# Second attention of a gated cross-attention stack: values and softmax sums in one product, normalised per query

## The chip, the cores and the metric

The kernel runs on one core of one Trainium2 chip. The metric is the device time of one execution in microseconds; lower is better. The engines are TensorE (PE in the profile; PEld is its weight load), VectorE (DVE), ScalarE (ACT), GpSimd (POOL) and SyncE (SP, which here only issues DMAs).

## The reference

Eight stages follow each other on x, of 16 items with 128 rows and 256 columns. Stages 0, 2, 4 and 6 are attentions over a context, stages 1, 3, 5 and 7 are feed-forward blocks; each adds its gated result to x. The change is in stage 2, the second attention:

```python
# q = layernorm(x), k = v = ctx_2048; per item B, rows D=128, columns L=256
qh = q.reshape(B, 8, 16, L)          # heads are groups of 16 ROWS
kh = k.reshape(B, 8, 16, L)
vh = v.reshape(B, 8, 16, L)
qk = jnp.einsum('bhdq,bhdl->bhql', qh, kh) / sqrt(16)
sm = jax.nn.softmax(qk, axis=-1)
ret = jnp.einsum('bhql,bhdl->bhdq', sm, vh).reshape(B, 128, L)
x = x + jnp.tanh(g_xattn[1]) * gamma * ret
```

So attention here runs between the 256 columns, and a head is 16 of the 128 rows. An item has 8 heads of 256 queries and 256 keys.

## The kernel before

The four compute engines and SyncE each run their own program, written out by hand, and wait on semaphores (`wait(name, item, k)` waits for the k-th signal of an item under that name). In stage 2 every engine walks the same loop, `s2_turns` (L2331): turns i = -3 to 17, and in one turn an engine handles several items at different steps. In names: b = i, p = i - 1, pp = i - 2, n = i + 3 on VectorE, GpSimd and SyncE, and n = i + 1 on TensorE.

An item goes through these steps:

- Preparation, for item n: VectorE combines the gathered rows of the stage before into x (L734) and takes the statistics (L772, L775). GpSimd makes the reciprocal deviation (L788, L790), normalises (L2385) and splits the result into three bf16 parts (`operands`, L804 to L812). SyncE stores the parts to `qscr` and loads them back as the operand `qop`, each of six combinations once (L2373), and the keys as `kop` (L2347). The keys of item n are loaded only after the key scores of item n - 3 are done. ScalarE scales gathered rows for a later item (`weigh`, L741), and GpSimd adds and gathers them (L748, L766).
- Maxima, for item b: TensorE makes scores by query in four steps (`scores`, L2540: 4 products each, two steps for each tile of 128 queries). VectorE takes each step's maxima per query and head (L2463), and splits the 16 maxima of a row into three bf16 parts (L804 to L812). TensorE transposes them into 24 rows of PSUM (L2600), and ScalarE copies these rows twice, for the even and the odd heads, into rows 96 to 119 of `qop` (L2516).
- Key scores, for item p: TensorE makes the scores again, keys on the partitions and with the maxima already subtracted, in four steps of 4 heads and 128 keys (`key_scores`, L2551). ScalarE takes the exponential of each step in two halves (L2504) into `PT`.
- Values, for item p: four steps (`values`, L2567). A step has 8 fp32 products of 128x32 by 128x256. Four of them multiply the exponentials with the values, laid out in `v2` as 32 columns of which 16 are those of a head and 16 are zero. The other four multiply them with `ones2`, 16 columns of ones, so that the sums stand in each of the 16 rows of a head. One product has two records in the trace. The even and the odd heads are added into one bank of PSUM: values in columns 0 to 255, sums in 256 to 511.
- End, for item pp: VectorE takes the reciprocal of the 128x256 sums (L2453) and multiplies the values with it and with the gate (L2459) into `q_tmp`. GpSimd adds `q_tmp` to x (L2406). x_done counts the items.

The order on each engine is fixed by the body of its loop. On TensorE one turn is: key scores 0 of p, scores 2 of b, key scores 1, values 0, scores 3, key scores 2, values 1, key scores 3, values 2, scores 0 of the next item, the transposes of the maxima of b (after a wait for them), values 3, scores 1 of the next item. On VectorE: maxima 0 and 1, preparation of n, the reciprocal of pp, maxima 2, the scaling of pp, maxima 3, the split of the maxima. On ScalarE: eight exponentials of p with the scaling of gathered rows behind the fourth, then both copies of the maxima of b. On GpSimd: the layout of the values of b (L2413, L2414, which waits for the values of b - 2), adding and gathering rows, deviation and normalisation of n, the addition for pp, the split of n. Behind the loop TensorE makes the context products of three items for stage 4 (L1295, L1298), which ScalarE copies (L1308, L1309). ScalarE then casts the weights w3h of stage 3 (L2176).

Two other places do what the change adds. In stage 0 ScalarE copies 128x512 of values and sums to `bc_sb` (L1023). In stage 4 TensorE transposes such a copy (L2962), and VectorE takes the reciprocal of 16 sums per row (L2776) and multiplies with it (L2778).

## Time and profile before

| | us |
|---|---|
| three runs | 1204.98, 1209.03, 1212.16 |
| median | 1209.03 |
| profiled execution | 1208.87 |
| its span, first to last instruction | 1207.1 |

| engine | busy, share of the span |
|---|---|
| TensorE, products | 86% |
| TensorE, weight loads | 67% |
| VectorE | 67% |
| GpSimd | 50% |
| ScalarE | 49% |

Busy shares are over all eight stages. The records of TensorE's products overlap, since one starts while the one before still runs out; its order and the distances of the starts say more than its busy time. Times in the rows are microseconds from the start of the span, where nothing else is said.

### The profile page before, as it was taken

To read this page: it belongs to the slowest core of one execution; us is meant where nothing else is said; L and a number is where in the kernel's file an instruction comes from. 1 tells how busy PE (TensorE), PEld (TensorE's weight loads), DVE (VectorE), ACT (ScalarE), POOL (GpSimd) and SP (SyncE) were. 2 spreads that over 40 slices of the span, in tenths; PEclk is the share of its full clock that TensorE was granted. 3 is DMA by queue.
4 is the path that set the end of the run, shared out by engine and by line. 5 is a ranking of instruction groups with operands and counts; after the bars stand their busy time and mean duration, and the time that the engine had idled before them with its cause. 6 is when DMAs were issued, how large, how long until landed. Compare 5 with 4: busy or idle time off the path is not lost.

```text
span 1207.1 us, 30765 instructions
## 1 busy us (share of the span) xinstructions
PE 1040.5 (86%) x11053; PEld 811.5 (67%) x11053; DVE 809.0 (67%) x2187; ACT 596.0 (49%) x1354; POOL 599.9 (50%) x1158
## 2 busy tenths in 40 slices
PE   4898899998687848888899979999978789879898
PEld 2576676766677724444577756777756589878898
DVE  2567666765555558888688875888765756745575
ACT  2455555655555347776621105777733544356432
POOL 2454656564688478874221114777643616600361
PEclk8899999999999969999999997999979989989999
DMA  5333333333566765544110011111021601244331
GB/s 181 98 99 103 102 99 100 121 125 126 182 210 204 177 166 143 145 135 115 41 70 0 1 42 31 35 36 35 4 87 51 212 2 62 80 124 154 105 113 60
DMA packets 110191, 119.85 MB, mean 99 GB/s; under 512 B 13373, under 2 KB 94485, under 8 KB 109789
## 3 DMA queue, kind: packets, MB, share of 16 engines
q1 hardware_dynamic: 96892, 89.65, 24.4%
q0 software_dynamic: 8256, 22.08, 6.2%
q10 hardware_dynamic: 4896, 6.20, 1.6%
q8 instruction: 89, 1.46, 0.5%
q14 instruction: 58, 0.47, 0.1%
HBM read 68.85 MB, written 49.03 MB: 98 GB/s over the span
## 4 chain that ended last, share of the span: by engine, by line
PE 50%; DVE 23%; issue 9%; DMA 7%; POOL 5%; ACT 4%; SPq 1%; ACTq 0%; POOLq 0%; DVEq 0%
PE psum L1125 4%; DMA PT<-xs 3%; DVE mx L2463 2%; DVE mx L888 2%; DVE x L2257 2%; PE psum L2567 2%; DVE mx L2764 2%; PE psum L1057 2%; PE psum L1758 2%; PE psum L1108 2%; PE psum L1760 2%; PE psum L1759 2%; PE psum L1059 2%; PE psum L1088 2%; PE psum L1969 2%
## 5 line engine op out<-in xcount | busy, mean ns | idle before, releaser
L888 DVE TENSOR_REDUCE mx<-psum 128x6 f32<-128x960 f32 (+3 forms) x80 | 80.7, 1008 | 65.4 <-PE psum L1093 64.3
L788 POOL TENSOR_SCALAR veps<-mv 128x1 f32<-128x1 f32 x112 | 28.8, 257 | 189.6 <-DVE mv L775 138.9
L766 POOL DMA_INDIRECT got<-ys,rows_y x64 | 63.9, 998 | 110.6 <-DMA ys<-yt 88.1
L975 ACT ACTIVATE PT<-psum 128x1024 f32<-128x1024 f32 x64 | 65.5, 1023 | 64.9 <-PE psum L1113 64.9
L2463 DVE TENSOR_REDUCE mx<-psum 128x4 f32<-128x1024 f32 x64 | 76.9, 1205 | 22.4 <-PE psum L2540 22.4
L2504 ACT ACTIVATE PT<-psum 128x512 f32<-128x512 f32 x128 | 69.5, 595 | 19.2 <-PE psum L2551 17.8
L1758 PE MATMUL psum<-xnTh,w7h 128*128 128x256 f32 x256 | 75.1, 293 | 1.3 <-issue 0.7
L1760 PE MATMUL psum<-xnTh,w7l 128*128 128x256 f32 x256 | 73.1, 286 | 0.0
L1759 PE MATMUL psum<-xnTl,w7h 128*128 128x256 f32 x256 | 73.0, 285 | 0.0
L2861 ACT ACTIVATE PT<-psum,mx 128x128 f32<-128x128 f32 x256 | 69.8, 396 | 5.1 <-DVE mx L2764 5.1
L790 POOL TENSOR_TENSOR rstd<-veps,minus_half 128x1 f32<-128x1 f32 x112 | 67.6, 604 | 9.3
L2567 PE MATMUL psum<-PT,arena 128*32 128x256 f32 x1024 | 70.0, 388 | 0.0
L1832 ACT ACTIVATE sil<-psum 128x256 f32<-128x256 f32 x64 | 24.5, 385 | 83.4 <-PE psum L1760 83.4
L2257 DVE SCALAR_TENSOR_TENSOR x<-psum,cw,x 128x256 f32<-128x256 f32 x128 | 52.4, 476 | 12.5 <-PE psum L2134 12.3
L1850 DVE TENSOR_TENSOR hTf<-sil,psum 128x256 f32<-128x256 f32 x64 | 26.7, 418 | 48.3 <-ACT sil L1832 48.0
L2132 PE MATMUL psum<-w3h,xnTh 128*128 128x512 f32 x128 | 53.1, 415 | 4.7 <-DVE x L2257 4.4
L2072 DVE TENSOR_TENSOR xTl<-psum,xTh 128x256 fp32r<-128x256 f32 x78 | 33.0, 424 | 31.8 <-ACT xTh L2043 31.1
L2868 ACT COPY arena<-psum 128x1024 f32<-128x1024 f32 x32 | 32.4, 1012 | 41.5 <-PE psum L2940 41.5
L1250 POOL COPY arena<-kv_f 32x64 f32<-32x64 f32 x160 | 38.7, 242 | 27.4 <-POOL arena L1250 22.1
L1969 PE MATMUL psum<-ident,PT 128*128 128x128 f32 x156 | 33.4, 297 | 21.6 <-DMA PT<-xs 20.2
L2085 DVE TENSOR_TENSOR ht<-silt,psum 128x128 f32<-128x128 f32 x78 | 22.4, 287 | 44.2 <-ACT silt L2055 43.9
L2134 PE MATMUL psum<-w3h,xnTl 128*128 128x512 f32 x128 | 50.9, 398 | 0.0
(445 smaller groups left out, 3473.7 us busy)
## 6 DMA issues: line engine op xcount, KB each, us to landing
xs<-qpad SPq DMA_DIRECT2D x34, 512.0 KB, 3.3
PT<-xs SPq DMA_DIRECT2D x78, 128.0 KB, 2.3
ys<-yt SPq DMA_DIRECT2D x78, 128.0 KB, 2.1
ext<-qscr SPq DMA_DIRECT2D x96, 64.0 KB
arena<-in_w SPq DMA_DIRECT2D x16, 320.0 KB, 3.0
w_raw<-in_w SPq DMA_DIRECT2D x12, 384.0 KB, 4.5
q_parts<-kscr SPq DMA_DIRECT2D x66, 64.0 KB, 2.4
kvd<-arena ACTq DMA_DIRECT2D x16, 256.0 KB, 2.7
```

The source lines that it names most:

```text
L766: pool.indirect_dma_start(out=dst[:, t % 4, k], out_offset=None, in_=ys[:], in_offset=bass.IndirectOffsetOnAxis(ap=rows_y[:, t, k:k + 1], ...
L790: nc.gpsimd.tensor_tensor(rstd[:, s], veps[:, s], minus_half[:], ALU.pow).then_inc(F("rstd").sem, 1)
L888: V.tensor_reduce(mx0[:, u0:u0 + m].rearrange("p j e -> p e j"), src, axis=AX.X, op=ALU.max, negate=True).then_inc(F("mx").sem, 1)
L975: A.activation(PT[:, 1024 * r:1024 * (r + 1)], bank(6, 2), ACT.Exp).then_inc(F("p").sem, 1)
L1758: MM(o, wh, xnTh[:, b % 2, c], start=(c == 0), stop=False)
L1759: MM(o, wh, xnTl[:, b % 2, c], start=False, stop=False)
L1760: t = MM(o, wl, xnTh[:, b % 2, c], start=False, stop=(c == NC - 1))
L2257: nc.vector.scalar_tensor_tensor(x[:, 2 * b + u], bank(2 + 2 * (j % 2) + u)[:, C * e:C * (e + 1)], cw[:, s, u, 2 * j + e:2 * j + e + 1], x ...
L2463: V.tensor_reduce(mx2[:, k // 2, 4 * (k % 2):4 * (k % 2) + 4], bank(4 - 4 * (k % 2), 2).rearrange("p (h l) -> p h l", h=4), axis=AX.X, op= ...
L2504: nc.scalar.activation(PT[:, 1024 * k + 512 * half:1024 * k + 512 * (half + 1)], bank(6 + half), ACT.Exp, scale=0.25).then_inc(F("p").sem, 1)
L2567: t = MM(bank(2 + s)[32 * m:32 * (m + 1), C * what:C * (what + 1)], g, PT[:, 1024 * k + 256 * m:1024 * k + 256 * (m + 1)], start=(k == 0 a ...
L2861: o = A.activation(p4[:, r, g], bank(4 + r)[:, 128 * g:128 * (g + 1)], ACT.Exp, bias=mx4[:, r, g:g + 1])
```

## The change

What it does, in stage 2 only:

- `v2` holds, for each head, 16 value columns and one column of ones, 17 in all; `ones2` is gone. A product takes 32 columns from the start of a head: its values, its ones, and 15 columns of what follows, which nobody reads. A value step has 4 products instead of 8. The even heads go to columns 0 to 255 of the bank, the odd ones to 256 to 511.
- ScalarE copies the bank to `bc_sb` when an item's values are done (`pvc`), TensorE transposes the copy in four pieces (`transpose_values`), so that queries stand on the partitions. VectorE takes the reciprocal of 16 sums per row and multiplies in two halves into `q_tmp` (`normalise_values`). TensorE transposes back in two pieces (`transpose_back`), and VectorE multiplies with the gate and adds to x in one instruction (`update`). GpSimd's addition is gone.
- Orders: TensorE has the transposes of pp behind key scores 0, values 0 behind scores 3, the transposes back behind values 1, and scores 0 of the next item ahead of values 2. It waits for x_done of pp ahead of the maxima transposes, which go to the same bank. ScalarE copies the maxima for the odd heads (e = 1) only behind the first two exponentials of the next turn; at the end of a turn stand the copy for the even heads and the new copy of the bank, which waits for the values of p. VectorE has `normalise_values` where the reciprocal was, and `update` behind the last maxima.

```diff
@@ GpSimd
-            P.memset(tail[:, 0:816], 0.0).then_inc(v2_ready, 1)
+            P.memset(tail[:, 0:576], 0.0).then_inc(v2_ready, 1)
...
+            P.memset(v2[:, :, :, :, 16:34:17], 1.0).then_inc(v2_ready, 1)
...
-            def add(p):
-                wait("on", p, 1)
-                P.tensor_tensor(x[:, p], x[:, p], q_tmp[:], ALU.add).then_inc(x_done.sem, 1)
...
-                P.tensor_copy(v2[:, s, :, :, 32:48], raw[:, :, :, 1]).then_inc(F("v").sem, 1)
+                P.tensor_copy(v2[:, s, :, :, 17:33], raw[:, :, :, 1]).then_inc(F("v").sem, 1)
@@ VectorE
-                V.reciprocal(bc_sb[:, 0:C], bank(2 + s)[:, C:2 * C]).then_inc(F("rden").sem, 1)
...
-                V.scalar_tensor_tensor(q_tmp[:], bank(2 + s)[:, 0:C], gg[:], bc_sb[:, 0:C], ALU.mult, ALU.mult).then_inc(F("on").sem, 1)
+            def normalise_values(p):
+
+                wait("pvT", p, 1)
+                pv = bank(2 + p % 2).rearrange("p (n w) -> p n w", w=32)
+                V.reciprocal(rden[:, 0:16].unsqueeze(2), pv[:, :, 16:17]).then_inc(F("rden").sem, 1)
+                wait("rden", p, 1)
+                for qt in range(2):
+                    t = V.tensor_tensor(q_tmp[:, 128 * qt:128 * (qt + 1)].rearrange("p (m e d) -> p e m d", m=4, e=2),
+                                        pv[:, 8 * qt:8 * qt + 8, 0:16].rearrange("p (e m) d -> p e m d", e=2),
+                                        rden[:, 8 * qt:8 * qt + 8].rearrange("p (e m) -> p e m", e=2).unsqueeze(3).to_broadcast([128, 2, 4, 16]), ALU.mult)
+                t.then_inc(F("on").sem, 1)
+
+            def update(p):
+                wait("oT_psum", p, 1)
+                V.scalar_tensor_tensor(x[:, p], bank(2 + p % 2)[:, 0:C], gg[:], x[:, p], ALU.mult, ALU.add).then_inc(x_done.sem, 1)
...
                 if inside(pp):
-                    reciprocals(pp, s)
+                    normalise_values(pp)
                 if inside(b):
                     maxima(b, 2)
+                    maxima(b, 3)
                 if inside(pp):
-                    scale(pp, s)
+                    update(pp)
                 if inside(b):
-                    maxima(b, 3)
@@ ScalarE
+                        if k == 0:
+                            copy_maxima(p, 1)
...
+                    copy_maxima(b, 0)
+                if inside(p):
+                    act.wait_ge(F("pv").sem, F("pv").at(p, 1))
+                    if p > 0:
+                        act.wait_ge(F("pvT").sem, F("pvT").at(p - 1, 1))
+                    nc.scalar.copy(bc_sb[:].rearrange("p (t e q) -> p e t q", t=2, e=2), bank(2 + p % 2).rearrange("p (e t q) -> p e t q", e=2, t=2)).then_inc(F("pvc").sem, 1)
@@ TensorE
-                for what in range(2):
-                    for m in range(4):
-                        g = (v2[:, s, lt, m] if what == 0 else ones2)[:, 16 * e:16 * e + 32]
-                        t = MM(bank(2 + s)[32 * m:32 * (m + 1), C * what:C * (what + 1)], g, PT[:, 1024 * k + 256 * m:1024 * k + 256 * (m + 1)],
-                               start=(k == 0 and what == 0), stop=(k == 3), skip_group_check=True)
+                for m in range(4):
+                    at = 288 * s + 34 * (4 * lt + m) + 17 * e
+                    t = MM(bank(2 + p % 2)[32 * m:32 * (m + 1), C * e:C * (e + 1)], tail[:, at:at + 32], PT[:, 1024 * k + 256 * m:1024 * k + 256 * (m + 1)],
+                           start=(k == 0), stop=(k == 3), skip_group_check=True)
...
+            def transpose_values(p):
+                wait("pvc", p, 1)
+                for r in range(4):
+                    t = nc.tensor.transpose(bank(2 + p % 2)[:, 128 * r:128 * (r + 1)], bc_sb[:, 128 * r:128 * (r + 1)], ident[:])
+                t.then_inc(F("pvT").sem, 1)
+
+            def transpose_back(p):
+                wait("on", p, 1)
+                for qt in range(2):
+                    t = nc.tensor.transpose(bank(2 + p % 2)[:, 128 * qt:128 * (qt + 1)], q_tmp[:, 128 * qt:128 * (qt + 1)], ident[:])
+                t.then_inc(F("oT_psum").sem, 1)
...
                 if inside(p):
                     key_scores(p, 0)
+                if inside(pp):
+                    transpose_values(pp)
                 if inside(b):
                     scores(b, 2)
                 if inside(p):
                     key_scores(p, 1)
-                    values(p, 1 - s, 0)
                 if inside(b):
                     scores(b, 3)
                 if inside(p):
+                    values(p, 1 - s, 0)
                     key_scores(p, 2)
                     values(p, 1 - s, 1)
+                if inside(pp):
+                    transpose_back(pp)
+                if inside(p):
                     key_scores(p, 3)
-                    values(p, 1 - s, 2)
                 if inside(n):
                     scores(n, 0)
+                if inside(p):
+                    values(p, 1 - s, 2)
                 if inside(b):
                     wait("mparts", b, 4)
+                    if inside(pp):
+                        pe.wait_ge(x_done.sem, NB + pp + 1)
```

## Rows read from the trace of the kernel before

**Rows 1.** Engines by stretch: busy us and instructions, granted clock, DMA share, GB/s.
```profile
430.00:445.00 15.00, 7.63 (x33) 3.84 (x34) 9.40 (x14) 5.07 (x10) 12.50 (x21) 0.50 0.70 208
...
500.00:540.00 40.00, 34.79 (x412) 18.62 (x404) 35.75 (x55) 28.94 (x50) 31.74 (x54) 1.00 0.48 135
```

**Rows 2.** Timeline of VectorE, one turn: start, duration, line, operation [idle before <-releaser].
```profile
504.02 1.23 DVE L2463 TENSOR_REDUCE mx<-psum 128x4 f32<-128x1024 f32 x1 [0.73 <-PE psum L2540]
...
506.28 1.76 DVE L2453 RECIPROCAL bc_sb<-psum 128x256 f32<-128x256 f32 x1
507.95 1.16 DVE L2463 TENSOR_REDUCE mx<-psum 128x4 f32<-128x1024 f32 x1
509.03 0.47 DVE L2459 SCALAR_TENSOR_TENSOR q_tmp<-psum,gg,bc_sb 128x256 f32<-128x256 f32 x1
509.42 1.21 DVE L2463 TENSOR_REDUCE mx<-psum 128x4 f32<-128x1024 f32 x1
510.67 0.21 DVE L804 CAST mxp<-mx 128x16 bf16<-128x16 f32 x1
```

**Rows 3.** Timeline of TensorE, the same turn.
```profile
502.30 0.22 PE L2600 MATMUL psum<-identb,mxp 128*24 128x128 bf16 x1 [0.86 <-DVE mxp L812]
...
503.37 0.61 PE L2540 MATMUL psum<-q_parts,ext 96*128 96x256 bf16 x4
...
512.00 0.22 PE L2600 MATMUL psum<-identb,mxp 128*24 128x128 bf16 x1 [0.86 <-DVE mxp L812]
```

**Rows 4.** Timeline of ScalarE, the same turn.
```profile
502.61 1.90 ACT L2516 COPY ext<-psum 24x1024 bf16<-24x1024 bf16 x2 [1.81 <-PE psum L2600]
504.54 2.24 ACT L2504 ACTIVATE PT<-psum 128x512 f32<-128x512 f32 x4
506.67 0.90 ACT L741 ACTIVATE got<-got,wk_all 128x256 f32<-128x256 f32 x2
```

**Rows 5.** Timeline of GpSimd, the same turn.
```profile
503.66 0.29 POOL L2413 COPY arena<-v_raw 128x128 f32<-128x128 f32 x1 [0.43 <-PE psum L2567]
...
509.77 0.73 POOL L2406 TENSOR_TENSOR x<-x,q_tmp 128x256 f32<-128x256 f32 x1
```

**Rows 6.** Timeline of TensorE, the maxima transposes of items 0, 1, 10 and 15.
```profile
442.21 0.37 PE L2600 MATMUL psum<-identb,mxp 128*24 128x128 bf16 x2 [1.12 <-DVE mxp L812]
...
453.58 0.23 PE L2600 MATMUL psum<-identb,mxp 128*24 128x128 bf16 x1
...
541.35 0.22 PE L2600 MATMUL psum<-identb,mxp 128*24 128x128 bf16 x1 [1.10 <-DVE mxp L812]
...
586.97 0.27 PE L2600 MATMUL psum<-identb,mxp 128*24 128x128 bf16 x2
```

**Rows 7.** Timeline of TensorE, the first context product behind the loop.
```profile
595.79 1.13 PE L1295 MATMUL psum<-PT,ctxT 128*128 128x256 f32 x4
```

**Rows 8.** Timeline of VectorE in stage 4: reciprocal of sums, a pair of products.
```profile
803.53 0.26 DVE L2776 RECIPROCAL rden<-psum 128x16 f32<-128x16 f32 x1
...
809.10 0.49 DVE L2757 TENSOR_TENSOR qpad<-q_tmp,rows 128x128 f32<-128x128 f32 x2
```

**Rows 9.** Timeline of TensorE in stage 4, four transposes of such a copy.
```profile
802.90 0.60 PE L2962 MATMUL psum<-ident,bc_sb 128*128 128x128 f32 x4
```

**Rows 10.** Instructions on the tile bc_sb: ns min/median/max, first and last start.
```profile
L1023 ACT COPY bc_sb<-psum x16: 585/585/586, 55.4 to 297.4; 128x512 f32<-128x512 f32 x16
```

**Rows 11.** Timeline of SyncE's queue, the query loads of one item.
```profile
512.36 2.80 SPq L2373 DMA_DIRECT2D ext<-qscr  x6
```

**Rows 12.** The page's DMA issues: KB each, median us from issue to landing.
```profile
q_parts<-kscr SPq DMA_DIRECT2D x66, 64.0 KB, 2.4
```

**Rows 13.** The chain of work that ended last: start, us, what.
```profile
602.65 1.05 ACT w3h L2176
```

**Rows 14.** Timeline of VectorE, the split's subtraction in items 10 and 13.
```profile
539.97 0.66 DVE L806 TENSOR_TENSOR mxr<-mx,mxp 128x16 f32<-128x16 f32 x1
...
568.68 0.17 DVE L806 TENSOR_TENSOR mxr<-mx,mxp 128x16 f32<-128x16 f32 x1
```

More of the change, by code:

```diff
@@ L191, in bass_program @@
         v_raw = sb("v_raw", [128, 2, 2 * 128])
-        v2 = tail[:, 0:768].rearrange("p (s l m w) -> p s l m w", s=2, l=2, m=4)
-        ones2 = tail[:, 768:816]
+        v2 = tail[:, 0:576].rearrange("p (s n) -> p s n", s=2)[:, :, 0:272].rearrange("p s (l m w) -> p s l m w", l=2, m=4)
         v2_ready = sem("v2_ready")
@@ L423, in bass_program @@
                              ("sq", 4, 0), ("mx", 4, 0), ("mparts", 4, 0), ("mxT_psum", 1, 0), ("mxT", 2, 0), ("st", 8, 0), ("p", 8, 0),
-                             ("pv", 1, 0), ("rden", 1, 0), ("on", 1, 0)])
+                             ("pv", 1, 0), ("pvc", 1, 0), ("pvT", 1, 0), ("rden", 1, 0), ("on", 1, 0), ("oT_psum", 1, 0)])
         sel2_in = sem("sel2_in")
@@ L2413, in lay @@
                 P.tensor_copy(v2[:, s, :, :, 0:16], raw[:, :, :, 0])
-                P.tensor_copy(v2[:, s, :, :, 32:48], raw[:, :, :, 1]).then_inc(F("v").sem, 1)
+                P.tensor_copy(v2[:, s, :, :, 17:33], raw[:, :, :, 1]).then_inc(F("v").sem, 1)
             def body(i, s):
-                pp, b, n = i - 2, i, i + 3
+                b, n = i, i + 3
                 def fetch_rows():
@@ L2434, in body @@
                         fetch_rows()
-                if inside(pp):
-                    add(pp)
                 if inside(n) and n >= 2:
@@ L2447, in wait @@
                 dve.wait_ge(F(n).sem, F(n).at(b, k))
-            def reciprocals(p, s):
-                wait("pv", p, 1)
-                if p > 0:
-                    wait("on", p - 1, 1)
-                V.reciprocal(bc_sb[:, 0:C], bank(2 + s)[:, C:2 * C]).then_inc(F("rden").sem, 1)
-            def scale(p, s):
-                wait("rden", p, 1)
-                if p > 0:
-                    dve.wait_ge(x_done.sem, NB + p)
-                V.scalar_tensor_tensor(q_tmp[:], bank(2 + s)[:, 0:C], gg[:], bc_sb[:, 0:C], ALU.mult, ALU.mult).then_inc(F("on").sem, 1)
+            def normalise_values(p):
+                wait("pvT", p, 1)
+                pv = bank(2 + p % 2).rearrange("p (n w) -> p n w", w=32)
+                V.reciprocal(rden[:, 0:16].unsqueeze(2), pv[:, :, 16:17]).then_inc(F("rden").sem, 1)
+                wait("rden", p, 1)
+                for qt in range(2):
[6 more added lines that the diff above has]
+                V.scalar_tensor_tensor(x[:, p], bank(2 + p % 2)[:, 0:C], gg[:], x[:, p], ALU.mult, ALU.add).then_inc(x_done.sem, 1)
             def maxima(b, k):
@@ L2496, in s2_act, with copy_maxima @@
             F = lambda n: f[2, n]
+            def copy_maxima(b, e):
+                act.wait_ge(F("mxT_psum").sem, F("mxT_psum").at(b, 1))
+                src = bank(2 + b % 2).bitcast(BF16)[0:24, 0:256].unsqueeze(1).to_broadcast([24, 4, C])
+                nc.scalar.copy(qop[96:120, b % 3].rearrange("p (m e) n -> p m e n", e=2)[:, :, e], src).then_inc(F("mxT").sem, 1)
             def body(i, s):
@@ L2512, in body @@
                 if inside(b):
-                    act.wait_ge(F("mxT_psum").sem, F("mxT_psum").at(b, 1))
-                    src = bank(2 + s).bitcast(BF16)[0:24, 0:256].unsqueeze(1).to_broadcast([24, 4, C])
-                    for e in range(2):
-                        nc.scalar.copy(qop[96:120, b % 3].rearrange("p (m e) n -> p m e n", e=2)[:, :, e], src).then_inc(F("mxT").sem, 1)
+                    copy_maxima(b, 0)
[4 more added lines that the diff above has]
+                    nc.scalar.copy(bc_sb[:].rearrange("p (t e q) -> p e t q", t=2, e=2), bank(2 + p % 2).rearrange("p (e t q) -> p e t q", e=2, t=2)).then_inc(F("pvc").sem, 1)
             s2_turns(body)
@@ L2560, in values @@
                     wait("mxT", p, 2)
-                    if p >= 2:
-                        wait("on", p - 2, 1)
                 wait("p", p, 2 * k + 2)
-                for what in range(2):
-                    for m in range(4):
-                        g = (v2[:, s, lt, m] if what == 0 else ones2)[:, 16 * e:16 * e + 32]
-                        t = MM(bank(2 + s)[32 * m:32 * (m + 1), C * what:C * (what + 1)], g, PT[:, 1024 * k + 256 * m:1024 * k + 256 * (m + 1)],
-                               start=(k == 0 and what == 0), stop=(k == 3), skip_group_check=True)
-                return t
+                for m in range(4):
+                    at = 288 * s + 34 * (4 * lt + m) + 17 * e
+                    t = MM(bank(2 + p % 2)[32 * m:32 * (m + 1), C * e:C * (e + 1)], tail[:, at:at + 32], PT[:, 1024 * k + 256 * m:1024 * k + 256 * (m + 1)],
+                           start=(k == 0), stop=(k == 3), skip_group_check=True)
+                return t
+            def transpose_values(p):
[8 more added lines that the diff above has]
+                t.then_inc(F("oT_psum").sem, 1)
             pe.wait_ge(v2_ready, 2)
@@ L2576, in body @@
             def body(i, s):
-                p, b, n = i - 1, i, i + 1
+                pp, p, b, n = i - 2, i - 1, i, i + 1
                 if n == 0:
```

2 lines of the change are left out of this document (removed).

## The prediction

> **What bounds the kernel now.** I read the page first (span, line groups), then the second attention, about 434 to 600 us: its engines by stretch [rows 1], the timelines of VectorE, TensorE, ScalarE and GpSimd over one turn of its loop [rows 2 to 5], and then the chain of work that ended last. A turn is the time from one pair of maxima transposes on TensorE (L2600) to the next, 502.30 to 512.00, so 9.70 us [rows 3]. From 500 to 540 us VectorE is busy 35.75 of 40 us, TensorE 34.79 (its records overlap, so this is no full load), GpSimd 31.74, ScalarE 28.94 [rows 1]. The turn's chain runs mostly through VectorE. Its one long wait is 0.73 us for the score product of L2540 [rows 2], which stands behind the last value step: L2600 starts at 502.30, the value step right after, the scores at 503.37 [rows 3]. So VectorE works some 8.97 of 9.70 us, and what is taken from it shortens the turn until something else is late.
>
> The marks of L2600 are at 442.21 for item 0, 453.58 for item 1, 541.35 for item 10, 586.97 for item 15 [rows 6]. That is 11.37 us for turn 1, 87.77 us for turns 2 to 10 (9.75 each), 45.62 for turns 11 to 15 (the last three have no new item to prepare), and 8.82 for turn 16, up to the context product L1295 at 595.79 [rows 7].
>
> **VectorE.** Removed per item: the 128x256 reciprocal, 506.28 to 507.95, so 1.67 us, and the scaling, 509.03 to 509.42, so 0.39 us [rows 2]. Added: a reciprocal of 128x16, 0.26 us in the fourth stage [rows 8]; I put 0.30 with the hand-over to what waits for it. Two 128x128 products; such a pair took 0.49 us [rows 8], less the overlap with the next instruction 0.42. An update of x out of PSUM; it has the form of the scaling that goes, so 0.39. Together 2.06 out and 1.11 in, 0.95 us less. The update also stands between the last maximum and the split, where the split's first cast waits for the maximum's result now: 509.42 to 510.67 is 1.25 us, against 1.08 from 507.95 to 509.03, where nothing waits [rows 2]. That gives 0.17 back.
>
> **TensorE.** Values and sums in one product: a value step falls from 8 products to 4. A step of 8 takes about 1.0 of the 1.07 us between L2600 and the scores [rows 3], so 0.5 us less a step, 2.0 a turn. The half of the last step stands right before the scores for which VectorE waits 0.73, so that wait falls to about 0.23. Added: four transposes of 128x128, 0.60 us to the last result [rows 9], and two, about half of that; they lie in TensorE's idle time.
>
> VectorE's turn is then 9.70 - 0.95 - 0.17 - 0.50 = 8.1 us. I walked the new turn to see who is late at that pace, with 0 at the maxima transposes:
>
> - ScalarE: first maxima copy at 0.31, as now (502.61 against 502.30 [rows 3, 4]). The pair takes 1.90 us, so one takes 0.95. Then the new copy of values and sums, 0.585 us by the same copy in the first attention [rows 10]; it waits for the last value step, ready at 0.63, so it doesn't wait. Then two exponentials (0.55 apart, four take 2.24), the second maxima copy, two exponentials, the two scalings of gathered rows (0.90), four exponentials [rows 4]. The first exponential starts at 1.85, the sixth ends at 6.85. Now both copies stand ahead of it and it starts at 2.24 (504.54 [rows 4]).
> - TensorE: the transposes of the values stand behind the first key scores and start when the copy is done, 1.95, and are done at 2.55. VectorE wants them at 3.48 (506.28 less 502.30, less the 0.5), so they are early by 0.9 us. The normalised values are ready at 4.3. The transposes back stand behind the second value step, which waits for the fourth exponential: done at 6.2, and VectorE comes for them at 6.4. That is 0.2 us of slack; behind VectorE's wait for them stand the update and the split, and behind the split the whole next turn.
> - The fourth key scores wait for the sixth exponential and run until 7.2, the next item's first scores until 7.6 (VectorE wants them at 7.9), then the third value step, and the next maxima transposes can start at 8.15. They also wait for the update, done at 6.9, so that wait costs nothing.
>
> So VectorE's own sequence (8.1) and the ring through ScalarE and TensorE (8.15) come out nearly alike. With both so close I take 8.3 us for turns 2 to 10, 8.2 for 11 and 12 (no scaling of rows on ScalarE). In 13 to 15 VectorE has no combination and statistics (504.02 to 506.28 less a maximum of 1.14, so 1.12 [rows 2]); its own turn is 7.0, and TensorE and ScalarE need some 7.6, 7.6 and 7.2.
>
> **GpSimd** loses the addition to x, 0.73 us [rows 5], and its wait. Its own turn is 9.70, less the 0.43 it idles for the value product [rows 5], less the addition (0.68 to the next): 8.6 us, more than 8.3. But it may fall behind: the split of an item is over before the value copy at 503.66 [rows 5], and its query loads go out at 512.36 [rows 11], 8.7 us later, with one store of a few us between. Nine turns at 0.3 are 2.7 us. I count nothing for it. The value copy has a stride of 17 where it had 32; I leave its two copies at 0.29 [rows 5].
>
> **SyncE.** Six key loads wait for the last key scores of an item, then six query loads follow; six issues take 2.80 us [rows 11], a load lands in 2.4 [rows 12]. The last lands about 7.6 us after those key scores and is wanted one turn less 0.2 later, 8.1: hidden, with 0.5 to spare. If not, it is up to 0.5 us a turn.
>
> **Turn 1** runs partly at the lower clock and loads a table; the exponentials no longer wait for both copies and the value steps are half as long. I take 1.5 us off (bounds 0 and 2.5).
>
> **The end.** Turn 16 saves about 0.5. But ahead of the three context products TensorE now waits for the last item's copy (0.6), its transposes (0.6), reciprocal and products (0.8), transposes back (0.3) and the hand-overs (0.3). That is 2.6 us in which it went on before. The chain of work runs through these products and then ScalarE's cast for w3h at 602.65 [rows 13], so I count all of it (bounds 0 and 3). x itself is finished about as early as before, since 1.67 us of reciprocal and GpSimd's 0.73 go from its path.
>
> **Sum.** 1.5 + (87.77 - 9 x 8.3 = 13.1) + (45.62 - 38.8 = 6.8) + 0.5 - 2.6 = 19.3 us less. The profiled execution took 1208.87 us (span 1207.1, 1.8 around it); the median of the runs is 1209.03, the same within 0.2. 1208.87 - 19.3 = 1189.6; I forecast 1190.
>
> **A rule weighed.** The split's small subtraction (128x16, both inputs in SBUF) took 0.66 us at 539.97, while GpSimd worked, and 0.17 at 568.68, while it did not [rows 14]. The Trainium skill ("SBUF — State Buffer", Who interferes with whom) tells that VectorE and GpSimd share a port pair held for a whole instruction, and that a VectorE operation with two SBUF inputs contends with GpSimd's reads. By it the new operations, with one PSUM input each, are safe, but GpSimd, busy nearly all of a new turn, would meet the split in every one. From the rows alone: a meeting costs up to 0.5 us, and the turn of rows 2 holds about half of that; over 12 turns this is +3 to -4.5 us around the sum.
>
> **Rivals.** (1) The ring doesn't hold its pace: the transposes back come late, VectorE idles at the update, and the next turn starts late by as much. At 9.0 us a turn 12 turns lose 8.5: 1198. For it speaks 0.2 us of slack, against it that ScalarE is busy only 28.94 of 40 us now [rows 1], 7.0 a turn, and gains 0.6. Chance 0.20. (2) GpSimd's 8.6 us is the pace of turns 2 to 10: +2.7, so 1193; against it its slacks above. 0.10. (3) The change doesn't do what it says: the transposes are not early, and VectorE waits in each turn for the whole new path. If that is 1.3 us in 12 turns, 15.6: 1206. Against it the 0.9 us above. 0.06. (4) Slower: TensorE's clock falls. It was granted 0.50 (1.2 GHz) from 430 to 445 us, where TensorE was busy 7.63 of 15 us, and 1.00 (2.4 GHz) later, where it was busy 34.79 of 40 [rows 1]. That is 8.4 us of a turn; less 2.0, with 0.7 of transposes, 7.1. At half clock it is 14.2, 5.9 us more than 8.3, so from four such turns on the kernel is slower than before; with eight it is 1237. Against it: 7.1 of 8.3 is the same share as now. 0.04. The Trainium skill ("TensorE: Matmul & The Clock Gate", HAM oscillation) tells of such a fall in kernels whose TensorE idles between bursts of products, as the end of turn 16 would have it.
>
> **How the numbers follow.** The forecast has the remaining 0.60, with 1184 to 1196 as its own range. For 8 in 10 the range reaches over rivals 1 and 2 and leaves out 3 and 4: 1183 to 1201. A measurement of this kernel can tell about 0.5%, 6 us. Faster by more: the forecast and rivals 1 and 2 less a little, 0.88; within it 0.07; slower 0.05.
>
> **What would show it.** Right: L2600 marks 8.3 us apart; VectorE's wait ahead of the second maximum near 0.2; value steps of 8 records in 0.5 us; no wait of VectorE at the new reciprocal; 2 to 3 us of idle TensorE ahead of L1295. Wrong: VectorE idle at the update (rival 1), at the reciprocal (3), GpSimd without idle time and others waiting for it (2), a clock under 1.00 after 460 us (4), or TensorE waiting for loads ahead of an item's first scores, which is SyncE.

## The result, and the profile after

| | before | after |
|---|---|---|
| runs | 4: 1204.98 to 1212.16 us | 4: 1186.44 to 1195.08 us |
| median | 1210.21 us | 1193.8 us |
| ratio of the medians | | 0.986 [0.982 to 0.990] |
| profiled execution | 1208.87 us, span 1207.1 | 1193.04 us, span 1191.2 |

The kernel is faster by 1.4%, 16 us; the forecast was 1190 with 1183 to 1201. Against the time of the profiled execution, which the sum was made for, 15.8 us went where 19.3 had been worked out.

The gain is in the loop of stage 2. The maxima transposes of item 0 start at 442.91 us (442.21 before [rows 6]), those of item 15 at 568.96 (586.97 before), the cast of w3h at 586.73 (602.65 before [rows 13]). From there to the end it is 604.47 us, against 604.45 before. So 16.6 us went between the transposes of item 0 and w3h, and 0.7 came back ahead of them. That the two ends agree so closely is in part chance. In three more profiles of kernels whose code is the same outside the end of stage 2 (after again and the two of "The end" below), item 0 starts at 441.01, 444.08 and 442.36 us, and from w3h to the end it is 605.55, 599.81 and 604.46 us. These stretches differ by 3 and by almost 6 us between executions, so whole times are compared by their medians, and what a change does in the stage by distances inside it.

Turn by turn, as distances between the maxima transposes (L2622 now):

| | before | forecast | after |
|---|---|---|---|
| turn 1 | 11.37 | 9.87 | 9.90 |
| turns 2 to 10 | 87.77 | 74.7 | 75.44 |
| turns 11 to 15 | 45.62 | 38.8 | 40.71 |
| item 15 to w3h | 15.68 | 17.8 | 17.77 |

Added up, 1.47 + 12.33 + 4.91 - 2.09 = 16.6 us, where 19.3 were forecast. Of the 2.7 us that are missing, 1.9 lie in turns 11 to 15 and 0.7 in turns 2 to 10.

The turns of after are 9.90, 8.25, 8.08, 8.99, 8.09, 8.84, 8.08, 8.76, 8.08, 8.27, 8.89, 8.30, 7.90, 7.81 and 7.81 us: one at 8.1, one at 8.8 to 9.0, and so on, until the last items have nothing to prepare.

VectorE's timeline over a fast turn, then the slow turn's wait (start, duration, idle before; the same stretch of before is [rows 2]):

```profile
462.34 1.22 DVE L2459 TENSOR_REDUCE mx<-psum 128x4 f32<-128x1024 f32 x1 [0.29 <-PE psum L2545]
463.48 0.41 DVE L733 TENSOR_TENSOR x<-x,got 128x256 f32<-128x256 f32 x1
463.93 0.43 DVE L771 BATCH_NORM_STATS2 stats<-x 128x6 f32<-128x256 f32 x1
...
464.60 0.23 DVE L2445 RECIPROCAL rden<-psum 128x16 f32<-128x16 f32 x1
464.86 0.49 DVE L2448 TENSOR_TENSOR q_tmp<-psum,rden 128x128 f32<-128x128 f32 x2
465.27 2.34 DVE L2459 TENSOR_REDUCE mx<-psum 128x4 f32<-128x1024 f32 x2
467.53 0.48 DVE L2455 SCALAR_TENSOR_TENSOR x<-psum,gg,x 128x256 f32<-128x256 f32 x1
467.93 0.16 DVE L803 CAST mxp<-mx 128x16 bf16<-128x16 f32 x1
...
511.55 1.23 DVE L2459 TENSOR_REDUCE mx<-psum 128x4 f32<-128x1024 f32 x1 [0.60 <-PE psum L2545]
```

Three things are to be seen: the reciprocal follows without a wait, the update follows without a wait, and what was 0.73 us of idle time ahead of the second maximum is 0.29 (0.29 to 0.41 over turns 2 to 12). From reciprocal to the next maximum it is 0.67 us where it was 1.67.

TensorE over the slow turn (compare [rows 3]):

```profile
503.14 0.22 PE L2622 MATMUL psum<-identb,mxp 128*24 128x128 bf16 x1
...
505.12 0.66 PE L2576 MATMUL psum<-ident,bc_sb 128*128 128x128 f32 x4
...
509.14 0.44 PE L2582 MATMUL psum<-ident,q_tmp 128*128 128x128 f32 x2
...
510.92 0.60 PE L2545 MATMUL psum<-q_parts,ext 96*128 96x256 bf16 x4 [0.52 <-issue]
511.44 0.64 PE L2569 MATMUL psum<-PT,arena 128*32 128x256 f32 x8
511.90 0.22 PE L2622 MATMUL psum<-identb,mxp 128*24 128x128 bf16 x1
```

A value step has 8 records now, and the maxima transposes start 0.46 us behind it. The transposes of the values end at 505.78, and VectorE comes for them at 506.75. The 0.52 us ahead of the first scores of the next item (L2545) are named "issue", so no compute engine released them; what is waited for there is an item's key and query loads. Before, TensorE had its waits elsewhere. Its waits between 450 and 560 us, in sum, times and the longest; before, then after:

```profile
PE psum L2600 <- DVE mxp L812: 9.3, 10, 1.1
PE psum L2551 <- ACT PT L2504: 4.7, 11, 0.4
```

```profile
PE psum L2545 <- issue: 2.9, 4, 1.0
PE psum L2622 <- DVE mxp L811: 0.4, 1, 0.4
```

TensorE no longer waits for VectorE's maxima; it waits for loads. The chain of work in 460 to 500 us, as shares by line, tells the same:

```profile
by line: PE psum L2556 18.5%; SPq L2345 15.0%; PE psum L2569 12.4%; DMA ext<-qscr 12.1%; PE psum L2545 10.7%; SPq L2371 8.3%; issue 8.2%; ACT ext L2497 7.6%; PE psum L2576 4.9%; PE psum L2582 1.8%; PE psum L2622 0.7%
```

VectorE is not in it. It runs through TensorE, one maxima copy on ScalarE, SyncE's issues and the landing of a load; SyncE and the load (L2345, L2371, DMA) are 35% of it.

### The profile page after: what moved, and what is told of

It is laid out like the page before. It is cut to its first block, busy times and chain, and to the rows that moved or that the text cites. A ratio compares the mean times of both kernels' runs of the same rounds, so it can differ in the third digit from the quotient of the medians.

```text
span 1191.2 us, 29919 instructions
## 1 busy us (share of the span) xinstructions
PE 1031.1 (87%) x10637; PEld 805.3 (68%) x10637; DVE 789.6 (66%) x2219; ACT 604.5 (51%) x1370; POOL 589.4 (49%) x1141
## 4 chain that ended last, share of the span: by engine, by line
PE 52%; DVE 20%; issue 8%; DMA 7%; POOL 6%; ACT 4%; SPq 2%; ACTq 0%; POOLq 0%; DVEq 0%
DMA PT<-xs 4%; PE psum L1124 4%; PE psum L2556 3%; DVE mx L887 2%; DVE mx L2786 2%; DVE x L2255 2%; PE psum L1056 2%; PE psum L2569 2%; PE psum L1757 2%; PE psum L1058 2%; PE psum L1107 2%; PE psum L1759 2%; PE psum L1758 2%; PE psum L1087 2%; PE psum L2130 2%
## 5 line engine op out<-in xcount | busy, mean ns | idle before, releaser
L787 POOL TENSOR_SCALAR veps<-mv 128x1 f32<-128x1 f32 x112 | 28.9, 258 | 202.9 <-DVE mv L774 134.9
L765 POOL DMA_INDIRECT got<-ys,rows_y x64 | 63.4, 991 | 113.4 <-DMA ys<-yt 89.4
L2459 DVE TENSOR_REDUCE mx<-psum 128x4 f32<-128x1024 f32 x64 | 76.6, 1217 | 17.8 <-PE psum L2545 17.8
L1757 PEld LDWEIGHTS psum<-xnTh,w7h 128*128 128x128 f32 x256 | 50.0, 195 | 1.5 <-issue 1.5
```

The source lines that it names most:

```text
L765: pool.indirect_dma_start(out=dst[:, t % 4, k], out_offset=None, in_=ys[:], in_offset=bass.IndirectOffsetOnAxis(ap=rows_y[:, t, k:k + 1], ...
L1757: MM(o, wh, xnTh[:, b % 2, c], start=(c == 0), stop=False)
L2459: V.tensor_reduce(mx2[:, k // 2, 4 * (k % 2):4 * (k % 2) + 4], bank(4 - 4 * (k % 2), 2).rearrange("p (h l) -> p h l", h=4), axis=AX.X, op= ...
```

## The experiments

All are built from the kernel after. Where no number of runs is given, a time is of one execution. For turns 2 to 12 the same code, profiled in four executions (after, after again, and two with another end), gave 92.63, 93.63, 93.96 and 92.79 us, so a difference under about 1.3 us there is none.

**Are the slow turns the loads'?** From item 3 on half of the key loads are left out.

```diff
-                for r in range(6):
+                for r in range(6 if n < 3 else 3):
                     sp.dma_start(kop[n % 3][16 * r:16 * (r + 1)], ...
...
-                    pe.wait_ge(k_in2[b % 3], b // 3 * 96 + 96)
+                    pe.wait_ge(k_in2[b % 3], b // 3 * 48 + 96)
```

> The changed kernel, with three of the six key loads of an item left out from item 3 on (the other key rows keep an older item's keys, so the result of the second attention is wrong; nothing else changes). In the changed kernel the maxima transposes of items 1 and 12 lie 92.63 us apart (11 turns). Theory L: in these turns the loads between an item's last key scores and the first scores three items later set the pace. Three issues of about 0.45 us less take 1.35 us off that path: the turns that took 8.8 to 9.0 become 8.1 to 8.3, the 11 turns 89 to 90, the kernel some 3 us faster. Theory G: GpSimd, 8.77 us a turn, sets the pace. Then nothing changes: 92.6.

Measured: 1188.65 us. Turns 2 to 12 took 92.0 us, turns 2 to 5 of them 8.08 to 8.13 each. TensorE's waits in 450 to 560 us:

```profile
PE psum L2622 <- DVE mxp L811: 2.1, 4, 0.8
PE psum L2556 <- ACT PT L2505: 1.0, 2, 0.6
```

The wait at L2545 is gone, so it is the loads'. The forecast of 89 to 90 us for the turns failed all the same: at 92.0 they are only 0.6 us below the lowest of the same code, which is within its spread. Something else took most of what the loads gave. Later turns are 8.76 and 8.67, and SyncE waits for GpSimd's split ahead of its store (L2365) for 15.7 us in 7 times, against 4.6 in 5 in after. That spoke for GpSimd.

**GpSimd's pace.** An addition of the size of the removed one is put back on GpSimd, which nobody waits for.

```diff
+                if inside(i - 2):
+                    pool.wait_ge(again.sem, i - 1)
+                    P.tensor_tensor(sil[:, 0], sil[:, 1], sil[:, 1], ALU.add).then_inc(again.sem, 1)
                 if inside(n) and n >= 2:
                     operands(P, pool, n, 1 - s)
```

> The changed kernel with one more GpSimd addition of 128x256 in each turn (on a spare tile, where the addition to x was), 0.7 us. Theory G (GpSimd is the pace of turns 2 to 10): every one of them is 0.7 longer from turn 2 on, 92.6 becomes about 99. Theory L (GpSimd only runs behind, and has about 6 us of slack at its hand-over to SyncE): turns 2 to 5 as without it, later ones up to 0.7 longer once the slack is used, 93 to 97 in all.

Measured: 1196.95 us, turns 2 to 12 in 96.45, as theory L had it. TensorE's wait for loads became 5.9 us in 6 times, the longest 1.6. GpSimd goes without idle time in both kernels; here are two of its starts at L787 in after:

```profile
504.05 0.29 POOL L787 TENSOR_SCALAR veps<-mv 128x1 f32<-128x1 f32 x1
...
512.83 0.27 POOL L787 TENSOR_SCALAR veps<-mv 128x1 f32<-128x1 f32 x1
```

That is 8.78 us. With the addition the same distance is 9.27 (503.50 to 512.77), more than the mean turn of 96.45 / 11 = 8.77, so GpSimd falls behind a little in each turn, and in later turns its split holds up the store and the loads (10.32, 9.24). SyncE waits for that split for 11.7 us here, against 4.6 in after. The same run tells what it was worth that the change took an addition from GpSimd: 2.5 to 3.8 us of turns 2 to 12, against the four executions of the same code.

**The same question from the other side.** GpSimd's addition of gathered rows (L747) is left out, so that only the first of two rows comes in, alone and with the halved key loads.

```diff
-            nc.gpsimd.tensor_tensor(got[:, t % 4, 0], got[:, t % 4, 0], got[:, t % 4, 1], ALU.add).then_inc(summed.sem, 1)
+            pool.sem_inc(summed.sem, 1)
```

> The changed kernel without GpSimd's addition of an item's two gathered rows (items 2 to 15 get only the first of them, so the results from there on are wrong). GpSimd's turn falls from 8.77 to about 8.0 us. With three key loads left out the first turns came down to 8.08 but the later ones stayed at 8.2 to 8.8. If those are GpSimd's lag, then here the turns from the eighth on lose it, while the alternation of the early turns (8.08, then 8.8 to 9.0), which is the loads', stays: 11 turns in 91 to 92. If GpSimd has no part in it: 92.6.

Measured: 1192.39 us, turns 2 to 12 in 94.56, no less than in after, where 91 to 92 had been expected if GpSimd had a part in them and 92.6 if not. SyncE no longer waits for GpSimd at all in 450 to 560 us, yet TensorE waits for the loads as before:

```profile
PE psum L2545 <- issue: 4.8, 6, 1.2
```

> Both: no addition of the gathered rows on GpSimd, and three of six key loads left out from item 3 on. If the loads and GpSimd's lag are all that keeps the turns above 8.1, the 11 turns between items 1 and 12 take 89 to 90 us (10 of 8.08, and one of 8.3). If VectorE's and TensorE's own ring is less regular than that, 91 or more.

Measured: 1190.06 us, turns 2 to 12 in 90.42, the lowest of all and 2.2 us below the lowest of the same code, with turns 2 to 9 at 8.07 to 8.26. It lies between the two expectations. TensorE waited for no load. So the loads are late by themselves, with GpSimd in time (the first of these two runs), and without them the pace of 8.08 holds turn after turn (the second). GpSimd's pace comes second: taking work from it shows, if at all, only once the loads are short (92.0 to 90.42, one execution each), and giving it more costs 3 us or so. Turns 10 to 12 still took 8.67, 8.47 and 8.46; there TensorE waits for VectorE's split (1.6 us in 3 times in 450 to 560 us).

**The halved value step.** Each product of a value step is issued twice, so that a step has its old length.

```diff
                 for m in range(4):
+                    for again in range(2):
                         t = MM(...)
```

> The changed kernel with every value product issued twice (values and sums are both doubled, so the result is the same): a step has 8 products again, 0.5 us more each. My walk has the second, third and fourth step on the ring: turns near 8.8 in turns 2 to 12 and in 13 to 15 (now 7.8). From the maxima transposes of item 0 to the first context product it takes 137.0 us now; expected 146 to 149. The rival, that the smaller product does not matter and the gain is VectorE's alone, gives 137 to 139.

Measured: 1205.73 us; item 0 to the first context product took 150.06 us, 13.05 more than in after (137.01), a little over what was expected. Most turns are 8.93 to 8.98; one is 10.78, with a wait of 1.7 us at L2545. VectorE's wait for the scores is back:

```profile
509.22 1.23 DVE L2459 TENSOR_REDUCE mx<-psum 128x4 f32<-128x1024 f32 x1 [1.09 <-PE psum L2545]
```

Of the 2.0 us that it puts on TensorE, 0.85 reach a turn (8.93 - 8.08). Turns 2 to 12 take 100.33 us, against 92.63 in after and 107.66 before the change. So the shorter value step is worth 7.7 us in them, and the rest of the change, VectorE's part and GpSimd's, 7.3. Over the whole stretch from item 0 to the first context product the rest is worth only 3.5 us (153.58 before, 150.06 here), since behind item 15 the new path costs 3.3 us without the shorter step and in turns 13 to 15 another 1.0. No run takes VectorE's part back alone.

**The maxima copies.** Both stand together again, ahead of the copy of values and sums.

```diff
                         if k == 0:
-                            copy_maxima(p, 1)
...
                     copy_maxima(b, 0)
+                    copy_maxima(b, 1)
```

> The changed kernel with both copies of the maxima rows at the end of a turn, as before the change, ahead of the copy of the values. By my walk the first exponential and the value transposes come 0.95 us later, of which ScalarE gives 0.6 back since the second copy no longer stands behind them: turns 0.3 to 0.4 longer, 137.0 us (item 0 to the first context product) becomes 140 to 143. If the place of the copy does not matter: 137.

Measured: 1199.32 us; item 0 to context 140.9 us, 3.9 more, inside the expectation. Most turns are 8.35 to 8.36 where the fast ones of after are 8.08, and waits appear that after doesn't have (TensorE's, in 450 to 560 us; then VectorE's at the update):

```profile
PE psum L2575 <- ACT bc_sb L2520: 11.7, 13, 0.9
```

```profile
511.33 0.48 DVE L2455 SCALAR_TENSOR_TENSOR x<-psum,gg,x 128x256 f32<-128x256 f32 x1 [0.32 <-PE psum L2581]
```

TensorE waits 0.9 us per turn for ScalarE's copy, and a third of that reaches VectorE. But turns 2 to 12 took 93.65 us together, inside the 92.63 to 93.96 of the same code: as the loads have more time in a turn of 8.35, TensorE's wait for them fell from 2.9 us to 0.7, and what the place of the copy gives in these turns the loads take back. The 3.9 us are 0.5 in turn 1, 1.0 in turns 2 to 12 (no more than the spread), 1.3 in turns 13 to 15 (8.28 each), which have no new item to load, and 1.1 behind item 15.

**The transposes early.** They stand behind scores 3 and not behind key scores 0.

```diff
                     key_scores(p, 0)
-                if inside(pp):
-                    transpose_values(pp)
...
                     scores(b, 3)
+                if inside(pp):
+                    transpose_values(pp)
```

> The changed kernel with the transposes of the values behind the fourth scores instead of behind the first key scores. In the changed kernel they end 0.97 us ahead of VectorE's reciprocal. Behind the fourth scores they end about 1.4 us later, so VectorE waits some 0.5 us a turn in turns 2 to 12 and 0.9 in 13 to 15; a part of the 0.5 goes into the wait that is there in every second turn. From item 0 to the first context product 137.0 us becomes 141 to 146. If early does not matter: 137.

Measured: 1197.61 us; item 0 to context 143.2 us, 6.2 more, as expected. Turns are 8.56 or more; turns 2 to 12 took 96.13 us, 2.2 above the highest of the same code. VectorE:

```profile
463.86 0.26 DVE L2445 RECIPROCAL rden<-psum 128x16 f32<-128x16 f32 x1 [0.64 <-PE psum L2576]
```

The reciprocal waits for the transposes, in sum 7.4 us in 13 times (450 to 560 us), where in after it waits 0.3 us.

**The end.** Two of the three groups of context products go into the last turn, around the last item's transposes.

```diff
+                if i == NB + 1:
+                    context_pe(pe, LATER[3][0])
                 if inside(pp):
                     transpose_values(pp)
+                if i == NB + 1:
+                    context_pe(pe, LATER[3][1])
...
-            for k in LATER[3]:
-                context_pe(pe, k)
+            context_pe(pe, LATER[3][2])
```

> The changed kernel with two of the three context products behind the loop put ahead of the last item's value transposes and of its transposes back, so that they fill TensorE's two waits (0.71 and 0.87 us) there. From item 0's maxima transposes to ScalarE's first cast of w3h it took 160.4 us before the change and takes 143.8 now. If the end of the stage hangs on the context products, as I forecast: 141.3 to 142.3, and the kernel 2 us faster. If it hangs on x of the last item, 143.8 or more.

Measured: 1189.11 us. TensorE behind the last value step, first in after, then here:

```profile
578.12 0.66 PE L2576 MATMUL psum<-ident,bc_sb 128*128 128x128 f32 x4 [0.71 <-ACT bc_sb L2521]
579.65 0.44 PE L2582 MATMUL psum<-ident,q_tmp 128*128 128x128 f32 x2 [0.87 <-DVE q_tmp L2448]
579.92 1.03 PE L1294 MATMUL psum<-PT,ctxT 128*128 128x256 f32 x4
```

```profile
579.98 1.13 PE L1294 MATMUL psum<-PT,ctxT 128*128 128x256 f32 x4
580.94 1.05 PE L1297 MATMUL psum<-ctxT,PT 128*128 128x128 f32 x8
581.83 0.60 PE L2576 MATMUL psum<-ident,bc_sb 128*128 128x128 f32 x4
582.27 1.03 PE L1294 MATMUL psum<-PT,o_n 128*128 128x256 f32 x4
```

Both waits are gone, and from item 15 to w3h it is 15.91 us and not 17.77: nearly all of the 2.1 us that the end had cost (15.68 before). The distance that the expectation was made for, item 0 to w3h, is 143.41 us, outside the 141.3 to 142.3 expected, as turns 2 to 12 took 93.96 here. To see whether the whole kernel has it, it was timed in five rounds beside after itself.

> The changed kernel once more, in the same rounds as the next one, to compare the two: 1191 to 1195 us, 0.984 to 0.988 of the kernel before.

> The changed kernel with two of the three context products ahead of the last item's transposes. In its trace the way from the last maxima transposes to the w3h cast fell by 1.86 us. If that stays in the whole time: 1.9 us, 0.16%, less than the changed kernel, 1189 to 1193.

| five rounds on one chip | runs | median | ratio to before |
|---|---|---|---|
| before | 11 | 1209.26 | |
| after again | 6: 1188.68 to 1196.33 | 1192.89 | 0.9863 [0.9836 to 0.9891] |
| contexts early | 6: 1190.10 to 1195.98 | 1193.17 | 0.9871 [0.9849 to 0.9894] |

The 1.9 us are there in the trace once more (item 15 to w3h 15.90 us against 17.84 in the profile of after again), and not in the medians, which differ by 0.28 us the other way, with six runs each that spread over 6 to 8 us. A gain of this size can't be told in the time, and whether it reaches the end of the kernel stays open; no version is claimed that beats after.

**Fewer, longer loads.** If the loads are late by SyncE's twelve issues, fewer should mend it: the scratch is laid out so that a load brings rows of 4 KB, two or three parts at once, three issues and not six for the keys and three for the queries (the stores become three each).

```diff
-                for r in range(6):
-                    sp.dma_start(kop[n % 3][16 * r:16 * (r + 1)], kscr[n, POS_K[r]].rearrange("(h d) n -> d h n", d=16)).then_inc(k_in2[n % 3], 16)
+                for part, r0, r1 in ((0, 0, 3), (1, 3, 5), (2, 5, 6)):
+                    src = kscr[n, part].rearrange("(d h) n -> d (h n)", h=8)
+                    if r1 - r0 > 1:
+                        src = src.unsqueeze(0).to_broadcast([r1 - r0, 16, 8 * C])
+                    sp.dma_start(kop[n % 3][16 * r0:16 * r1].rearrange("p h n -> p (h n)"), src).then_inc(k_in2[n % 3], 16)
```

The second of the two kernels that follow has the early context products of "The end" as well.

> The changed kernel with another layout of the parts in HBM (rows of a head's same place together), so that an item's key and query operands come with three loads each instead of six and with rows of 4 KB instead of 512 B; its parts are stored with three stores instead of one. Theory L: the 11 turns between items 1 and 12 fall from 92.6 to about 89.5, and 3 us come off the kernel, if the stores of the keys in the stage before cost nothing there. Theory G: 92.6, no gain.

> Both edits, merged loads and early context products: the two gains lie at different places and add up, about 5 us less than the changed kernel, 1188 to 1189 us. If the stage is held by something else, 1192 to 1194.

Measured: 1243.64 and 1242.07 us, some 50 us slower. Both expectations failed. The chain of merged_loads (start, us, what):

```profile
516.63 0.42 SPq L2378
...
517.10 9.49 DMA ext<-qscr
526.59 0.09 issue
526.68 1.01 PE psum L2552 x4
```

The same step in the chain of after:

```profile
519.19 0.31 SPq L2345
...
523.81 0.43 SPq L2371
524.24 0.04 issue
524.28 2.58 DMA ext<-qscr
526.86 0.37 PE psum L2556 x2
```

SyncE saved its issues, and the load then took 9.5 us to land and not 2.6. The DMA engines by stretch, of the loads' last three microseconds in merged_loads and of the landing in after (the last two columns are their busy share and GB/s, ahead of them TensorE's clock):

```profile
523.40:526.40 3.00, 0.00 (x0) 0.00 (x0) 0.17 (x1) 0.22 (x1) 1.75 (x3) 0.85 0.25 84
```

```profile
524.30:526.80 2.50, 2.42 (x24) 0.73 (x16) 2.50 (x3) 2.49 (x6) 2.17 (x5) 1.00 0.58 144
```

TensorE stands still, VectorE and ScalarE nearly (0.17 and 0.22 us of 3), GpSimd works 1.75, and a quarter of the 16 DMA engines are busy, so about four at a time. A cause that fits is stated by the Trainium skill ("DMA: Bandwidth & Descriptors", Rules for kernel authors): a DMA whose outermost dimension is shorter than 16, such as a leading broadcast of c copies, is confined to at most c engines. The merged key loads have such a dimension, of 3 and of 2, and the query loads go out behind them. The trace agrees. Counted in its DMA packets, those of 4 KB on SyncE's queue run 3.1 at a time from 520.5 to 522 us, 2.0 from 509.5 to 511.5, and 1.0 at 512; in between, as from 517.5 to 519, they run 15 to 16 at a time. But no run here had the long rows without that dimension, so that this alone makes the landing long is not shown. In 450 to 560 us TensorE waits 45.1 us for the loads in 5 times: 28.6 of it ahead of item 0, whose transposes come at 461.2 us, 18 us later than in after, and 16.5 in four turns of the loop. This experiment changed more than the issues and so tells nothing on them; that the loads are late rests on the halved keys.

## Why the prediction was right, point by point

**VectorE bounds before, and what is taken from it shortens the turn: held, and then it stopped being the bound.** The new operations measured 0.23 us for the reciprocal (0.30 put), 0.49 less overlap for the products, 0.48 for the update (0.39 to 0.40 to the next instruction), as put. The wait for scores fell to 0.29 to 0.41 where 0.23 was forecast: in a turn of 8.08 VectorE now has time left. Not in the sum was a gain in the split: its three small operations behind the first cast (subtraction, cast, subtraction) took 0.31, 0.40 and 0.24 us in the mean before and take 0.22, 0.23 and 0.19 now (450 to 562 us), together 0.3 us less. The row for the middle cast, before and after (ns, lowest, median and highest):

```profile
L810 DVE CAST mxp<-mxr x12: 174/528/530, 452.0 to 560.6; 128x16 bf16<-128x16 f32 x12
```

```profile
L809 DVE CAST mxp<-mxr x14: 174/174/633, 450.0 to 560.6; 128x16 bf16<-128x16 f32 x14
```

The prediction had weighed this contention after the Trainium skill ("SBUF — State Buffer", Who interferes with whom) and feared that a GpSimd busy all the time would meet each split. What GpSimd does at that moment decides it. Before, its own split's subtraction ran beside the middle cast in seven of twelve turns, and the cast ended 0.03 us behind it, as a port pair held for a whole instruction would have it:

```profile
511.12 0.53 DVE L810 CAST mxp<-mxr 128x16 bf16<-128x16 f32 x1
510.93 0.69 POOL L806 TENSOR_TENSOR xres<-xn,xparts 128x256 f32<-128x256 f32 x1
```

Now GpSimd is busy there too, but mostly with issuing a gather (L765), beside which six of eight such casts took 0.17 to 0.18 us (the others 0.24 and 0.41):

```profile
510.57 0.18 DVE L809 CAST mxp<-mxr 128x16 bf16<-128x16 f32 x1
510.46 1.08 POOL L765 DMA_INDIRECT got<-ys,rows_y  x1 [0.17 <-issue]
```

Nothing in the change aimed at this; it is luck, worth 0.3 us of VectorE's turn. The new operations, which read PSUM, kept one length, 0.47 to 0.48 for the update.

**The ring through ScalarE and TensorE at 8.15: held.** An undisturbed turn takes 8.08. Its chain (461.07 to 469.14 us) is the first maxima copy on ScalarE, 1.01 us, and TensorE's own sequence for all the rest; the exponentials, which the walk had on the ring, are not in it. Two pieces that keep it short were moved: the value step (8.93 without it) and the copy between the halves of the maxima rows (8.35 without it, though the loads hide that in turns 2 to 12).

**The transposes early by 0.9 us: held.** They were early by 0.97 (505.78 against 506.75). Moved back, they cost 6.2 us, with 7.4 us of waits at the reciprocal. The transposes back were closer than forecast: they end at 467.49 and 509.58 us, the update starts at 467.53 and 509.67, so 0.04 and 0.09 us ahead and not 0.2.

**Loads hidden, with 0.5 to spare: failed.** This is the step of the mechanism that the forecast got wrong, and the reason for a turn that is now fast and now slow. "The last lands about 7.6 us after those key scores": from the chain of after it is 519.19 to 526.86, 7.67 us, so that was right where a load lands in 2.6. But "is wanted one turn less 0.2 later, 8.1" was for a turn of 8.3; at the pace that the ring holds it is wanted at 7.9, and the median landing of the key loads rose from 2.4 us to 2.8 in 500 to 540 us, and from 2.4 to 3.2 in 460 to 500 (over the whole page 2.4 [rows 12] and 2.9; the query loads of after: 2.7). Hardly anything is to spare. A turn that waits gives the next one the time, which is why they alternate. It cost 0.15 to 0.9 us in a slow turn, 75.44 - 9 x 8.08 = 2.7 us in turns 2 to 10. That these turns came out near the forecast all the same, 75.44 for 74.7, is luck: the 8.3 had an allowance of 0.15 us a turn because VectorE and the ring were close, which did not cost anything, and the loads, which had none, used it up and 0.7 us more. The sentence behind it, "if not, it is up to 0.5 us a turn", holds for the mean, 0.3. The halved keys showed the cause by the wait that went, and together with GpSimd's shorter turn by the time as well. Why a load lands later now is open; in 500 to 540 us the DMA engines' busy share went from 0.48, at 135 GB/s [rows 1], to 0.65 at 155:

```profile
500.00:540.00 40.00, 37.07 (x344) 19.17 (x343) 35.51 (x70) 34.85 (x61) 33.92 (x59) 1.00 0.65 155
```

**GpSimd may fall behind without cost: held in turns 2 to 10, unclear behind.** Its own turn was 8.73 to 9.00, 8.85 in the mean of nine (8.6 forecast). It goes without idle time, but TensorE waits for loads as much when its work is cut.

**Turns 11 to 15: mis-sized by 1.9 us.** 8.2, 8.2, 7.6, 7.6 and 7.2 were forecast, 8.89, 8.30, 7.90, 7.81 and 7.81 measured. The first is a turn that waits for loads. In the last three, 1.1 us together, the term that was mis-sized is "TensorE and ScalarE need some 7.6, 7.6 and 7.2". In turns 13 and 14 the chain is again TensorE's own sequence and the first maxima copy, and that takes 7.8 to 7.9 us. VectorE is ready earlier and waits for the transposes back:

```profile
559.81 0.48 DVE L2455 SCALAR_TENSOR_TENSOR x<-psum,gg,x 128x256 f32<-128x256 f32 x1 [0.76 <-PE psum L2582]
```

In turn 14 this wait costs nothing, as TensorE doesn't wait for VectorE's split behind it. In turn 15, where TensorE has no next item's scores, it does, and there the mechanism of rival 1 is at work, for 0.37 of the 7.81 us:

```profile
568.96 0.22 PE L2622 MATMUL psum<-identb,mxp 128*24 128x128 bf16 x1 [0.37 <-DVE mxp L811]
```

In turns 2 to 10 VectorE has no wait at the update.

**Turn 1 and the end: held, turn 1 with luck.** 1.47 us off for 1.5, and 2.09 on for 2.1. In the three other profiles of the same loop turn 1 took 9.06, 9.28 and 8.98 us and not 9.90, which would be 2.1 to 2.4 us off. The end's 2.1 us are TensorE's waits of 0.71 and 0.87 and the transposes, and early context products take 1.86 of them away in the stage.

**The clock (rival 4): didn't come.** It was granted 1.00 (2.4 GHz) in 500 to 540 us, with TensorE busy 37.07 of 40. In 445 to 460 us, where turn 1 ends, it was 0.78 and had been 0.84; in the three other profiles it was 0.93, 0.80 and 0.91, so the 0.78 can't be put down to the change. In 460 to 500 us it was 1.00 too, and 0.96 in one of the three others.

## What to carry to other kernels

When a change takes work from the bounding engine, work out each other path at the new pace, not the old one: a queue with half a microsecond to spare at a turn of 8.3 us had next to none at 8.08. A new path through three engines can be nearly free inside a loop when each piece is done before its next user comes, though behind the loop, where nothing covers it, it shows (here 2.1 us). Each such place can be tested by moving that piece alone; look at the single turns as well as at the sum, since a second limit, here the loads, can hide the cost. Halve a load to ask whether it is late, before changing how it is issued, and read the answer from the wait, not from one total.

## What the runs showed of the hardware

- Query loads in rows of 4 KB (64 to 192 KB, to 16, 32 or 48 partitions), behind key loads with a leading broadcast of 3 and of 2 copies, landed 9.4 to 9.7 us after SyncE's last issue (four turns of merged_loads); those of 64 KB in rows of 512 bytes, to 16 partitions, in 2.7. At the end of the landing a quarter of the DMA engines were busy, and the 4-KB packets ran 3, 2 or 1 at a time for whole microseconds.
- The median landing of an unchanged key load grew from 2.4 us to 2.8 when the bytes per us rose by 15% (500 to 540 us, 135 to 155 GB/s).
- A small VectorE cast between SBUF tiles took 0.53 us beside GpSimd's subtraction of two SBUF tiles and mostly 0.17 to 0.18 beside GpSimd's issue of a gather; a change of what they met, with nothing changed in the operations, was worth 0.3 us a turn.
